# Transposing the normalized input: from DMA transposes to TensorE transposes, with half of the residual scaling moved into the first expert

## The reference

```python
xn = layernorm(x)                       # over the 1024 numbers of a token
x  = x + attention(xn) + ffn(xn)
# attention: c_q, c_kv = xn @ W_DQ, xn @ W_DKV (32 wide), k_r = xn @ W_KR (32 wide)
#            8 heads of 128 + 32, softmax over 2048 keys, output @ W_O
# ffn:       scores = xn @ router_w.T, gates by three Sinkhorn steps, the best 2 of 8 experts
#            return xn + sum over experts of gate * ((relu(xn @ wg) * (xn @ wp)) @ wo)
```

## Time and profile before

| what | value |
|---|---|
| time, median of 2 runs | 4070.95 us (4063.54 and 4078.36) |
| the profiled execution, its own time | 4077.32 us |
| its span on the slowest core (core 2) | 4075.8 us |
| spans of the other cores | 4011.7 to 4059.4 us |
| PE busy, share of the span | 3549.0 us, 87% |
| DVE, ACT, POOL busy | 800.7, 743.7, 728.0 us |

### The profile page before, as it was taken

How to read it: one execution, slowest core, us unless ns; L and a number is a source line. 1 busy time by engine, 2 the same in 40 slices (tenths; PEclk the granted TensorE clock), 3 DMA queues, 4 the chain that set the end, 5 groups by cost and what they waited for, 6 DMA issues and landing times.

```text
span 4075.8 us, 42792 instructions; the slowest of 8 cores (4011.7 to 4075.8 us)
## 1 busy us (share of the span) xinstructions
PE 3549.0 (87%) x14785; PEld 1451.3 (36%) x15082; DVE 800.7 (20%) x1146; ACT 743.7 (18%) x1211; POOL 728.0 (18%) x1038
## 2 busy tenths in 40 slices
PE   1119999999999999988888888999999999999998
PEld 0004344444434344422222222344444444444443
DVE  1102121121212112112222222221121212112121
ACT  1212010110101010034444444110101101010010
POOL 1002222222222222200000000022222222222221
PEclk9559999999999999987788878999999999999999
DMA  4116888978788797820000000177878787787877
GB/s 62 45 38 61 107 79 106 104 81 114 72 106 79 105 103 82 112 36 1 1 1 1 0 1 1 42 68 109 96 91 109 78 114 72 110 102 85 113 74 134
DMA packets 638821, 294.85 MB, mean 72 GB/s; under 512 B 567820, under 2 KB 567853, under 8 KB 638614
## 3 DMA queue, kind: packets, MB, share of 16 engines
q0 software_dynamic: 610624, 271.03, 57.0%
q1 hardware_dynamic: 27990, 21.07, 1.8%
HBM read 550.39 MB, written 8.39 MB: 137 GB/s over the span
## 4 chain that ended last, share of the span: by engine, by line
PE 80%; DMA 5%; DVE 5%; SPq 4%; ACT 3%; issue 3%; POOL 0%; DVEq 0%; ACTq 0%; POOLq 0%
PE psum L622 21%; PE psum L562 20%; PE psum L554 20%; PE psum L785 4%; PE psum L781 4%; DMA s_areaC<-wexp 3%; SPq L337 3%; DVE s_resid L644 3%; PE psum L771 3%; PE psum L775 3%; PE psum L816 1%; ACT s_areaB L791 1%; PE psum L673 1%; DMA s_xnT<-s_areaB 1%; PE psum L354 1%
## 5 line engine op out<-in xcount | busy, mean ns | idle before, releaser
L622 PE MATMUL psum<-s_areaC,s_areaA 128*128 128x512 bf16 x4013 | 937.8, 391 | 113.9 <-DVE s_resid L644 74.0
L554 PE MATMUL psum<-s_xnT,s_wgbuf 128*128 128x512 bf16 x4010 | 959.1, 379 | 25.5 <-DVE s_resid L644 16.4
L562 PE MATMUL psum<-s_xnT,s_wpbuf 128*128 128x512 bf16 x4019 | 960.4, 379 | 4.1
L573 ACT ACTIVATE s_areaB<-psum 128x512 bf16<-128x512 f32 x512 | 305.7, 597 | 2464.1 <-PE psum L554 2463.8
L517 POOL DMA_DIRECT2D s_wgbuf<-wg x256 | 224.9, 878 | 2420.7 <-PE psum L554 2349.6
L622 PEld LDWEIGHTS psum<-s_areaC,s_areaA 128*128 128x128 bf16 x4096 | 407.0, 100 | 642.4 <-issue 195.1
L580 DVE TENSOR_TENSOR s_areaA<-s_areaB,psum 128x512 bf16<-128x512 bf16 x512 | 351.8, 687 | 1351.9 <-PE psum L562 1346.1
L554 PEld LDWEIGHTS psum<-s_xnT,s_wgbuf 128*128 128x128 bf16 x4096 | 399.0, 98 | 506.7 <-issue 28.5
L562 PEld LDWEIGHTS psum<-s_xnT,s_wpbuf 128*128 128x128 bf16 x4096 | 400.8, 98 | 483.3
L603 POOL DMA_DIRECT2D s_areaC<-wexp x512 | 272.5, 540 | 683.1 <-PE psum L622 681.4
L791 ACT ACTIVATE s_areaB<-psum 128x512 bf16<-128x512 f32 x512 | 305.7, 597 | 431.1 <-PE psum L785 399.9
(11 more groups left out here) (110 smaller groups left out, 674.9 us busy)
## 6 DMA issues: line engine op xcount, KB each, us to landing
s_areaC<-wexp POOLq DMA_DIRECT2D x512, 256.0 KB, 6.6
s_wgbuf<-wg POOLq DMA_DIRECT2D x256, 256.0 KB, 4.7
s_wpbuf<-wp POOLq DMA_DIRECT2D x256, 256.0 KB, 5.7
s_resid<-x SPq DMA_DIRECT2D x16, 512.0 KB, 4.2
y<-s_resid SPq DMA_DIRECT2D x1, 4096.0 KB, 11.7
y<-s_resid SPq DMA_DIRECT2D x2, 2048.0 KB, 7.7
s_xnT<-s_areaB SPq DMA_TRANSPOSE x128, 2.4
s_areaC<-wo_attn POOLq DMA_DIRECT2D x1, 2048.0 KB, 16.1
```

What stands on the lines that cost most here:

```text
L554: w.do("tensor", lambda t, c_=c, tb_=tb, tt2_=tt2, gs_=gs, b_=gb: t.matmul(bank(b_)[:, :], S["wgbuf"].ap()[:, gs_, c_, :], S["xnT"].ap()[: ...
L562: w.do("tensor", lambda t, c_=c, tb_=tb, tt2_=tt2, gs_=gs, b_=pbk: t.matmul(bank(b_)[:, :], S["wpbuf"].ap()[:, gs_, c_, :], S["xnT"].ap()[ ...
L573: w.do("scalar", lambda s, b_=gb, sl_=gp_count % 2: s.activation(out=Ebuf[:, sl_, :], in_=bank(b_)[:, :], func=AF.Relu), inc="sS")
L622: w.do("tensor", lambda t, f_=f, dh_=dh, tt_=tt, bk_=bk, ws_=ws, tb_=tb: t.matmul(bank(bk_)[:, :], hbuf[:, f_, tt_ * 128:(tt_ + 1) * 128], ...
```

## The change

Three things, with `statc` and the queues otherwise as they were (line numbers of the changed kernel are up to 22 higher):

- The DMA transposes go. For each of the 8 blocks of a tile, TensorE transposes the block out of `xnbf` into PSUM bank 0 or 1 in turn (L337 of the changed kernel), against the identity `eyeb`, and VectorE copies the bank into `xnT` (L342). A transpose waits for the copy two before it, a copy for its transpose. ScalarE's wait for a free `xnbf` slot is now for TensorE's transposes of the tile two before. The matmuls of the group wait for the last copy.
- The semaphore `qtr` goes, and with it the wait at the start of each half of the experts.
- The overwriting of `resid` stays where it was for the groups 0 and 1. For the groups 2 and 3 (tiles 8 to 15) it moves into the first expert, after the slices ft 8 to 15, one tile each, on the same engine as before.

```diff
                     if i >= 2:
-                        w.wait("scalar", "qtr", 128 * (i - 1))
+                        w.wait("scalar", "tS", tok[("tr_t", i - 2)])
...
-                    if j < 2:
...
+                    if B < 2:
+                        if j < 2:
...
-                    w.wait("sync", "sS", tok[("xn_s", i)])
-                    w.wait("sync", "qtr", 128 * i)
+                    w.wait("tensor", "sS", tok[("xn_s", i)])
                     for c in range(8):
-                        w.do("sync", lambda q, c_=c, i_=i, sl_=sl: q.dma_start_transpose(
-                            S["xnT"].ap()[:, c_, i_ * 128:(i_ + 1) * 128],
-                            xnbf[:, sl_, c_ * 128:(c_ + 1) * 128]), inc="qtr", k=16)
+                        b = (i * 8 + c) % 2
+                        w.wait("tensor", "vS", bank01[b])
+                        w.do("tensor", lambda t, c_=c, b_=b, sl_=sl: t.transpose(
+                            bankb(b_)[:, 0:128], xnbf[:, sl_, c_ * 128:(c_ + 1) * 128],
+                            S["eyeb"][:]), inc="tS")
+                        tk = w.tok("tS")
+                        w.wait("vector", "tS", tk)
+                        w.do("vector", lambda v, c_=c, b_=b, i_=i: v.tensor_copy(
+                            S["xnT"].ap()[:, c_, i_ * 128:(i_ + 1) * 128], bankb(b_)[:, 0:128]), inc="vS")
+                        bank01[b] = w.tok("vS")
+                        tok[("trev_v", i * 8 + c)] = w.tok("vS")
+                    tok[("tr_t", i)] = w.tok("tS")
...
-                w.wait("tensor", "qtr", 128 * (4 * (tn + 1)))
+                w.wait("tensor", "vS", xready)
...
-                w.wait("tensor", "qtr", 128 * NT)
...
+                        if tb == 0 and e == 0 and 8 <= ft < NT:
+                            i_t, bp_, j_ = ft, (ft // 4) % 2, ft % 4
+                            if j_ < 2:
+                                w.wait("vector", "sS", tok[("xn_s", i_t)])
+                                w.do("vector", lambda v, i2=i_t, b2=bp_, j2=j_: v.tensor_scalar(
+                                    S["resid"].ap()[:, i2, :], S["resid"].ap()[:, i2, :],
+                                    stw[:, b2, j2, 0:1], stw[:, b2, j2, 6:7],
+                                    ALU.mult, ALU.add), inc="vS")
...
+                            else:
+                                w.wait("scalar", "vS", tok[("cols_v", ft // 4)])
+                                w.do("scalar", lambda s, i2=i_t, b2=bp_, j2=j_: s.activation(
+                                    out=S["resid"].ap()[:, i2, :], in_=S["resid"].ap()[:, i2, :],
+                                    func=AF.Identity, bias=stw[:, b2, j2, 6:7],
+                                    scale=stw[:, b2, j2, 0:1]), inc="sS")
...
```

More of the change, by code:

```diff
@@ L25 @@
 BF = ml_dtypes.bfloat16
-SEM_NAMES = ["qc", "qk", "x0", "x1", "qo", "qtr",
+SEM_NAMES = ["qc", "qk", "x0", "x1", "qo",
              "wg0", "wg1", "wg2", "wp0", "wp1", "wp2",
@@ L334, in walk @@
-                    w.wait("sync", "sS", tok[("xn_s", i)])
-                    w.wait("sync", "qtr", 128 * i)
-                    for c in range(8):
-                        w.do("sync", lambda q, c_=c, i_=i, sl_=sl: q.dma_start_transpose(
-                            S["xnT"].ap()[:, c_, i_ * 128:(i_ + 1) * 128],
-                            xnbf[:, sl_, c_ * 128:(c_ + 1) * 128]), inc="qtr", k=16)
+                    if B < 2:
+                        if j < 2:
+                            w.wait("vector", "sS", tok[("xn_s", i)])
+                            w.do("vector", lambda v, x_=xtile, j_=j, i_=i: v.tensor_scalar(
+                                S["resid"].ap()[:, i_, :], x_, stw[:, bp, j_, 0:1],
+                                stw[:, bp, j_, 6:7], ALU.mult, ALU.add), inc="vS")
+                            tok[("resid_v", i)] = w.tok("vS")
+                        else:
+                            w.do("scalar", lambda s, x_=xtile, j_=j, i_=i: s.activation(
+                                out=S["resid"].ap()[:, i_, :], in_=x_, func=AF.Identity,
+                                bias=stw[:, bp, j_, 6:7], scale=stw[:, bp, j_, 0:1]), inc="sS")
+                            tok[("resid_v", i)] = w.tok("sS")
@@ L340, in walk @@
+                    tok[("tr_t", i)] = w.tok("tS")
                 i = B * 4 + 3
                 tn = B
-                xready = None
+                xready = tok[("trev_v", i * 8 + 7)]
                 if tn == 0:
@@ L589, in do_ffn_tb @@
                             filler.pop(0)()
+                        if tb == 0 and e == 0 and 8 <= ft < NT:
[6 more added lines that the diff above has]
+                                    ALU.mult, ALU.add), inc="vS")
+                                tok[("resid_v", i_t)] = w.tok("vS")
+                            else:
+                                w.wait("scalar", "vS", tok[("cols_v", ft // 4)])
[3 more added lines that the diff above has]
+                                    scale=stw[:, b2, j2, 0:1]), inc="sS")
+                                tok[("resid_v", i_t)] = w.tok("sS")
                     tok[("gp_done_v", tb, e)] = w.tok("vS")
```

## The result

| what | value |
|---|---|
| ratio to before | 0.9706, 95% interval 0.968 to 0.9733: faster |
| this ratio of 4070.95 us | 3951.3 us (3940.7 to 3962.2), 119.7 us less |
| median of all 11 runs, the disturbed ones too | 3956.05 us |
| the profiled execution, its own time | 3939.37 us |
| its span on the slowest core (core 5) | 3937.8 us (other cores 3909.2 to 3935.1) |

Some executions of either kernel were disturbed (the cores of one die at a lower granted clock), and the ratio leaves them out; so it, and no plain median, is set against the forecast of 3952 us.

A forecast was written before the change was run, and what follows sets the result against it. A chain of latencies, SyncE's issue of DMA transposes, was taken to bound the input stage: 186.6 us of stretches become 66.4, gain 120.2, less 0.9 gives 119.3, from median 4070.95 to 3952 us; range 3925 to 3983.

The forecast's parts named there:

- part 2: Input stage: TensorE transposes and VectorE copies through two banks cost 0.44 us per block, copy 0.29, 16.0 us per group.
- The DMA transposes bound the stage, at the price of their issue: Input stage: SyncE issues one transpose every 1.28 us; removing all 128 ends four stretches of 186.6 us together.
- rival A: VectorE's copy out of PSUM moves two elements at a time, 0.227 us; 4.0 us less, 3948; chance 0.20.
- the 16 to 17.5: Sign in the changed kernel's profile: us from a group's first normalized tile to its first matmul, in place of 46.7.
- Overwriting of `resid` among the copies, 1.2 us in the groups 0 and 1: Input stage, VectorE: overwriting loses its cover, delaying copies by 0.4 and 0.8 us; 17.2 us in each of these groups.
- Nothing from the loads of x, and the rest of a group left alone: Input stage: freed loads still wait for sums, worth 0; the other 22 to 24 us of each group's period stay.
- One overwriting is not hidden, 0.9 us behind the gates: First expert: seven of eight moved overwritings hide under TensorE; that of ft 9 lengthens the 2.39 us wait by 0.9.
- B, the clock coming up: Input stage: TensorE reaches full clock, matmuls (35.8 us now) give back 8 us, transposes 3; 3941; chance 0.07.
- half clock through all projections: Input stage: half clock through each group's 32 matmuls costs 19 us more, 3971; chance 0.06 shared with the hand-off rival.
- C, the hand-off between tiles: Input stage: TensorE waits for ScalarE at every tile, 23 us more, 3975; chance 0.06 shared with half clock.
- D, later work giving the gain back: After the input stage: the slowest core fares worse at lower clock by about 40 us, 3992; chance 0.04.
- E, a dear round trip: Loop of two banks: slower than before if a block costs over 1.40 us; at 1.5 4083 us; chance 0.03.

## Why the prediction was right or wrong

The time came out at 3951.3 by the ratio, for 3952 forecast, and the experiments bear out the mechanism. What failed is a size, that of the copy in part 2. By its parts:

1. *The DMA transposes bound the stage, at the price of their issue:* right. Without them the stretches fall from 186.6 to 62.4; with half of them a stretch is 26.7.
2. *The loop of two banks, 0.44 per block:* the loop is as told, one wait of each engine for two blocks, but a block takes 0.405. **The term that was mis-sized is the copy:** 0.29 taken, 0.225 measured. I had both bounds and took the nearer in width, and the value that rival A worked out, 0.227, was the true one. 66.4 us for the four stretches became 62.4, rival A's 4.0, and the stretches of the groups 2 and 3, 15.2, lie below the 16 to 17.5 that the prediction named as its sign. The run with a float32 bank shows the cause: 292 ns, and 67.0 us for the four.
3. *Overwriting of `resid` among the copies, 1.2 us in the groups 0 and 1:* right, and a little large. Groups with it take 15.97 and 16.15, without it 15.16; put back into the last two groups it costs 1.15 in each.
4. *Nothing from the loads of x, and the rest of a group left alone:* right. The two slowest cores alone mislead here: core 2 before and core 5 after make the rest of the four periods 80.9 and 83.4 us and the first tile 0.7 later. Over all eight cores the rest hardly changes: the 24 projections take 28.6 us for 28.9 in the four groups together, and the first normalized tile starts at 46.3 for 47.7 (means). The second group's projections begin at a granted clock of 0.50 in both kernels (before, core 2: 0.50 from 163.6 to 166 us). The experts begin at 190.1 for 314.2, 124.1 us earlier, of which the stretches are 122.4 (in the kernel before they sum to 186.6 us on the even cores and to 183 on the odd ones). On the even cores, from one of which the forecast took its 186.6, the stretches give 124.2, 4 more than the 120.2 forecast; that is the copy's error.
5. *One overwriting is not hidden, 0.9 us behind the gates:* right, 3.31 for 2.39, with and without the rest of the change.
6. *The waits on `qtr`:* nothing was seen of them.

That the total agrees to 0.7 us is luck: the interval of the ratio is 10.8 us to either side, wider than the error of 4, which only the traces show.

The rivals. A, the copy at two elements at a time, is what happens. The Trainium skill, page "VectorE: DVE Perf Modes", section "Why PSUM operands drop a tier", says so of 16-bit operands in PSUM, and the runs agree: 225 ns against 292. B, the clock coming up, didn't happen, and half clock through all projections didn't either (24 at half clock would take 10.4, they took 7.2 to 8.2). (B's 35.8 us of matmuls counted 23 of the third group's 24; all 24 take 8.08, which makes it 36.0.) The rule that I cited against B, from the Trainium skill, page "TensorE: Matmul & The Clock Gate", section "PE-mode transpose", gave the right outcome for a wrong reason: ordinary matmuls in the same loop stay at 0.50, and 32 transposes per tile reach 1.00. So it was not the kind of instruction that held the clock down. Whether the gaps between them did or their number, no run separates, since the extra transposes changed both. The measurement decides, against the page. C, the hand-off between tiles, is refuted: TensorE waits for ScalarE only four times. D, later work giving the gain back: from the experts' first matmul to the end the cores' median was 3732 us before and is 3738 after, the slowest core 3761 and 3744. The run that moves the overwritings alone, whose later work is that of the kernel before but for their 0.9 us, has a median of 3739, so 7 us is what one profile differs from another, and not a loss of 40 (by the prediction's own working D would have been 35: a spread of 64.1 less a lag of 29.3). That the profiled spans differ by 138 us and not by 121 is this slowest core's 17. E, a dear round trip, is refuted: 0.405 per block, not 1.40.

## What to carry to other kernels

Price a stage of latencies by the step of its slowest queue, and look for the same loop elsewhere in the trace: the value projection gave the changed loop to 9%, though neither of its instructions was there. Then ask what the round trip is for: eight 128-column bf16 blocks fit one bank, and one copy for eight halves the stretch again (15.2 to 7.5 us); after it the order of the statistics is worth as much again (0.9616 to 0.9543, where the packing brought 0.9706 to 0.9634). A one-sided bound on an operation's type (float32 in PSUM for bf16 in PSUM) is a term to state both ways: its error, 4 us here, is hidden in the noise of the ratio, and only the trace shows it. And a part of a stage is compared on all cores, not on the slowest core of each kernel, which need not be the same one.

## What the runs showed of the hardware

- A copy of 128 columns out of PSUM takes VectorE 225 ns for bf16 and 292 ns for float32; 1024 columns of bf16 take 692 ns. So eight small copies cost 1800 ns for what one does in 692, before any hand-over.
- Eight transposes in a row into one bank take 1.01 us at granted clock 0.50, where eight in the loop of two banks take 3.2 with their copies.
- With 32 transposes per tile the granted clock goes from 0.51 to 1.00 within the second group, as with 24 of them replaced by ordinary matmuls. In the loop of two banks, one block every 0.4 us, it stays at 0.50 in the groups 1 to 3, for transposes and ordinary matmuls alike.
- A wait that goes is not a gain of its size: ScalarE's waits for the loads of x fell by 19.5 us, and the stage by 6.
